# Two hidden units of the second feed-forward block placed ahead of the first block's output units at the head of each step

## The chip, the cores and the metric

The kernel runs on one NeuronCore of a Trainium2 chip. The metric is the device time of one execution in microseconds (us). Before the change the median of three executions is 3286.47 us (3281.36 to 3291.28).

## The reference, cut to what matters

Two layers run over an image batch `x` of 16 x 96 x 96 x 96 (images, channels, rows, columns). Each layer has a mixer on the image and then a feed-forward block (FFN) on its tokens:

```python
# layer 0
x = x + _L0_conv_ref(_ln_c(x), ...)
t = _to_tokens(x)
t = t + _L0_ffn_ref(_ln_t(t), W1, b1, W2, b2)
# layer 1
x = x + _L1_conv_ref(_ln_c(x))
t = t + _L1_ffn_ref(_ln_t(t), W1, b1, W2, b2)

def _ffn_ref(x, W1, b1, W2, b2):
    h = relu(_qlinear(x, W1, b1))     # 96 -> 384 hidden
    return _qlinear(h, W2, b2)        # 384 -> 96
def _qlinear(x, W, b):
    y = q_acc(einsum('bsk,nk->bsn', q_mul(x), q_mul(W)))   # operands in 8 bit, sums in 16 bit
    return q_acc(y + q_mul(b))
```

The mixer of layer 0 compares every 3 x 3 patch with 512 vectors (the scores), takes the best match and sends it through a small multilayer network (the MLP). The mixer of layer 1 divides by a power of a 5 x 5 window sum.

## The kernel before, in words

The image is cut into 128 tiles of 128 patches with 9 pixels each, eight tiles to an image. All engines walk through the same list of 145 **steps**, and in one step each engine works on several tiles at different stages (`PARTS`, line 63): the scores of tile k+3 (`f1`), the match of k+2 (`f2`), the MLP of k+1 (`f3`), the first layer of FFN 0 of tile k (`back`), its second layer for tile k-1 (`tail`), the input of FFN 1 for tile k-11 (`pre`) and both layers of FFN 1 for tile k-12 (`rear`). Nothing is scheduled by a program: the order in which each engine does its part of a step is written out by hand in the `body` functions, TensorE's at lines 488 to 545 and ScalarE's at lines 623 to 681. An engine works strictly in that order, so an instruction that waits holds back everything written after it. Every eighth step (k % 8 = 1) window sums are added and in the one after it VectorE computes the factors of an image.

One FFN tile is 11 **units** on TensorE, numbered 0 to 10 (`fill`, line 379). Units 0 to 8 are hidden units: one matrix product each (line 393), of 512, 512 and 128 columns in turn. Units 9 and 10 are the output units: 15 and 12 products (line 401) that need the finished hidden tile. Each FFN owns two banks of PSUM and unit u uses bank u % 2. ScalarE copies each unit out (`take`, line 565): hidden units to `ffn_hid`, output units to `ffn_y` (both line 553). A unit may be filled when the unit two before it has been copied out.

Three things gate an FFN tile. ScalarE writes the normalised input `ffn_x` (`norm`, line 586). SyncE's queue (SP) then issues a DMA that transposes it into `ffn_xT` (`turn`, line 331); unit 0 waits for it to land (line 387). VectorE adds bias and ReLU to the hidden tile in three parts (line 898) and rounds it (line 906, the **round-up**); the first output unit waits for that (line 398). For FFN 1 the input of a tile is written near the end of step k-1, the transpose is issued there, behind the store of an output tile (line 348) and the loads of the next `xt` (line 325) and `xc` (line 318), and the hidden units run in step k. For FFN 0 the hidden units run at the end of step k-1, the round-up is VectorE's last work of that step, and the output units run at the head of step k.

At the head of a step TensorE does, in this order: two scores (line 416), FFN 0's unit 9, one score, FFN 1's unit 0, FFN 0's unit 10, FFN 1's units 1 and 2, then the transpose of the MLP's input (line 434). ScalarE copies that to `inpT`; `win_turn` (line 423) and `mlp_in` (line 439) wait for `inpT`, and from there on TensorE goes in one row through scores, `mlp_mid` (lines 445 and 447), `win_scores` (line 429) and the rest of FFN 1's hidden units to `mlp_last` (line 453), `conv` (line 461) and FFN 0's hidden units. ScalarE also computes `x3` at the head (`lrn_pixels`, line 599, nine pixels in a step), and its copies of the units stand in an order of their own between these.

Of the kernel before, what the change touches and what calls it, by code (L numbers as in the profile page):

```python
# [116 lines left out]
def build(nc, x_tok, x_chan, wm_in, wi1_in, wi1r_in, wi2_in, wl1_in, wl2_in, wconv_in, bmlp_in, ffn_in, shift_in,  # L117
# [4 lines left out]
    with ctx:  # L122
# [116 lines left out]
        ffn0, ffn1 = Ffn("ffn0", 0, 4), Ffn("ffn1", 1, 6)  # L239
# [121 lines left out]
        def _(pe):  # L361
# [44 lines left out]
            def score(f1, f2, p, j0, j1):  # L406


                if j0 == 0:
                    pe.wait_ge(xc_loaded[p], landed(f1, p))  # L410
                for j in range(j0, j1):

                    pe.wait_ge(score_taken, f1 * J + j + (2 if j == WIN_TURN else 1))
                    if j == WIN_TURN + 1 and f2 is not None:
                        pe.wait_ge(vidx_ready, f2 + 1)
                    last = pe.matmul(ps_score[score_bank(j)], xc[p][:, j, :], wcT[:, :], start=True, stop=True)  # L416
                    last.then_inc(score_ready, 1)

            def win_turn(f2, p):
                pe.wait_ge(win_loaded, (f2 + 1) * 16)  # L420
                wait_past(pe, winT_ready, f2)
                wait_past(pe, inpT_ready, f2)
                pe.transpose(ps_a[0:C, 0:P], win[p][:, :], ident[:, :]).then_inc(win_turned, 1)
# [7 lines left out]
            def mlp_turn(f3):  # L431
                pe.wait_ge(inp_ready, f3 + 1)
                wait_past(pe, x1_ready, f3)
                pe.transpose(ps_a[0:D1, 0:P], inp[:, :], ident[:, :]).then_inc(inp_turned, 1)
# [53 lines left out]
            def body(k):  # L488
                def scores(j0, j1):
                    if k.f1 is not None:  # L490
                        score(k.f1, k.f2, k.q, j0, j1)

                def hidden_units(ffn, tile, first, units):
                    if tile is not None:
                        fill(ffn, tile, k.back_p if ffn is ffn0 else k.rear_p, first, units)

                def out_units(ffn, tile, parity, u):
                    if tile is not None:
                        fill(ffn, tile, parity, HC * G + u, 1)

                scores(0, 2)
                out_units(ffn0, k.tail, k.tail_p, 0)
                scores(2, 3)
                hidden_units(ffn1, k.rear, 0, 1)
                out_units(ffn0, k.tail, k.tail_p, 1)
                hidden_units(ffn1, k.rear, 1, 2)
                if k.f3 is not None:
                    mlp_turn(k.f3)
                hidden_units(ffn1, k.rear, 3, 1)
                if k.f2 is not None:  # L510
                    win_turn(k.f2, k.q)
                if k.lrn is not None:
                    pe.wait_ge(box_ready, k.lrn + 1)
                if k.f3 is not None:
                    mlp_in(k.f3)
                hidden_units(ffn1, k.rear, 4, 1)
                scores(3, WIN_TURN)
                if k.f3 is not None:
                    if k.f2 is not None:
                        pe.wait_ge(winT_ready, k.f2 + 1)  # L520
                    mlp_mid(k.f3)
                hidden_units(ffn1, k.rear, 5, 1)
                if k.f2 is not None:
                    win_scores(k.f1, k.f2)
                hidden_units(ffn1, k.rear, 6, 1)
                scores(WIN_TURN, 5)
                hidden_units(ffn1, k.rear, 7, 1)
                scores(5, 6)
                if k.f3 is not None:
                    mlp_last(k.f3)  # L530
                scores(6, 7)
                hidden_units(ffn1, k.rear, 8, 1)
                if k.f3 is not None:
                    conv(k.f3)
                hidden_units(ffn0, k.back, 0, 2)
                scores(7, 8)
                hidden_units(ffn0, k.back, 2, 3)
                scores(8, J)
                window_sums(k, 0, 5)
                hidden_units(ffn0, k.back, 5, 2)  # L540
                out_units(ffn1, k.rear, k.rear_p, 0)
                window_sums(k, 5, 10)
                hidden_units(ffn0, k.back, 7, 2)
                out_units(ffn1, k.rear, k.rear_p, 1)
                window_sums(k, 10, WINDOW_PARTS)

            steps(body)


        @block.scalar  # L550
        def _(act):
# [39 lines left out]
            def lrn_pixels(k, j0, j1):  # L591

                if k.pre is None:
                    return
                if j0 == 0:
                    act.wait_ge(cols_ready, k.pre + 1)
                    wait_past(act, x4_ready, k.pre - XT + 1)
                for j in range(j0, j1):
                    last = nc.scalar.activation(x3[:, k.pre3, j, :], x2[:, k.pre & RING - 1][:, j, :],  # L599
                                                ACT.Identity, bias=cols[k.q][:, 1, j:j + 1],  # L600
                                                scale=cols[k.q][:, 0, j:j + 1])
                if j1 in (XA, J):
                    last.then_inc(x3_ready, 1)
# [19 lines left out]
            def body(k):  # L623
                def take_hidden(ffn, tile, first, units):
                    if tile is not None:
                        take(ffn, tile, k.back_p if ffn is ffn0 else k.rear_p, first, units)

                def take_out(ffn, tile, parity, u):
                    if tile is not None:
                        take(ffn, tile, parity, HC * G + u, 1)  # L630

                lrn_pixels(k, 0, 3)
                take_out(ffn0, k.tail, k.tail_p, 0)
                lrn_pixels(k, 3, 4)
                take_hidden(ffn1, k.rear, 0, 2)
                if k.f3 is not None:
                    act.wait_ge(inp_turned, k.f3 + 1)
                    copy(inpT[:, :], ps_a[0:D1, 0:P]).then_inc(inpT_ready, 1)
                take_hidden(ffn1, k.rear, 2, 2)
                take_out(ffn0, k.tail, k.tail_p, 1)  # L640
                if k.f2 is not None:
                    act.wait_ge(win_turned, k.f2 + 1)
                    copy(winT[0:C, :], ps_a[0:C, 0:P]).then_inc(winT_ready, 1)
                if k.f3 is not None:
                    act.wait_ge(z1_made, k.f3 + 1)
                    nc.scalar.activation(h[:].rearrange("c m p -> c (m p)"), ps_b[0:C, 0:M1 * P], ACT.Relu,
                                         scale=1.0 - LEAK).then_inc(h_ready, 1)
                take_hidden(ffn1, k.rear, 4, 1)
                norm0(k, 0, 5)
                take_hidden(ffn1, k.rear, 5, 1)  # L650
                if k.f3 is not None:
                    act.wait_ge(z2_made, k.f3 + 1)
                    nc.scalar.activation(vcs[:, :], ps_a[0:C, 0:P], ACT.Tanh,
                                         bias=bmlp[:, 0:1]).then_inc(vcs_ready, 1)
                norm0(k, 5, 7)
                take_hidden(ffn1, k.rear, 6, 1)
                norm0(k, 7, 8)
                take_hidden(ffn1, k.rear, 7, 1)
                if k.f3 is not None:
                    act.wait_ge(z3_made, k.f3 + 1)  # L660
                    for q in range(2):
                        last = nc.scalar.activation(h1[0:LH, q, :], ps_b[0:LH, q * P:(q + 1) * P], ACT.Relu,  # L662
                                                    bias=bmlp[0:LH, 1 + q:2 + q])
                    last.then_inc(h1_ready, 1)
                norm0(k, 8, J)
                take_hidden(ffn1, k.rear, 8, 1)
                lrn_pixels(k, 4, XA)
                norm1(k, 0, 1)
                lrn_pixels(k, XA, 6)
                norm1(k, 1, 3)  # L670
                lrn_pixels(k, 6, 8)
                norm1(k, 3, 4)
                take_hidden(ffn0, k.back, 0, 2)
                lrn_pixels(k, 8, J)
                take_hidden(ffn0, k.back, 2, 3)
                norm1(k, 4, XA)
                norm1(k, XA, 6)
                take_hidden(ffn0, k.back, 5, 4)
                norm1(k, 6, J)
                take_out(ffn1, k.rear, k.rear_p, 0)  # L680
                take_out(ffn1, k.rear, k.rear_p, 1)

            steps(body)


# [576 lines left out]
```

## Time and profile before

| what | value |
|---|---|
| median of three executions | 3286.47 us |
| the profiled execution, its own time | 3290.14 us |
| span of its trace | 3288.4 us |
| TensorE busy (share of the span) | 2775.2 us (84%) |
| VectorE busy | 2900.0 us (88%) |
| ScalarE busy | 2642.5 us (80%) |
| GpSimd busy | 1511.8 us (46%) |
| mean granted TensorE clock | 0.962 |

The rows of the trace name the engines PE (TensorE matrix products), PEld (its weight loads), DVE (VectorE), ACT (ScalarE), POOL (GpSimd) and SP (SyncE, which issues most DMAs). `out<-in` are the program's names with buffer numbers left out: `banks` is PSUM, `x` stands for several pixel tiles, `ffn_x`, `ffn_xT`, `ffn_hid` and `ffn_y` for those of either FFN. A time in brackets is idle time of the engine just before the row and what ended it. Products overlap in the pipeline, so the distance from one start to the next says more than a row's length. The granted clock is a share of 2.4 GHz: 1.00 is that, 0.50 is 1.2 GHz.

### The profile page before, as it was taken

The page shows a single profiled execution, that of the slowest core. Times are in us where ns is not written, and L with a number is a line of the kernel's source. Part 1 is how long each engine was busy: PE and PEld are TensorE (multiplying, and loading weights), DVE is VectorE, ACT ScalarE, POOL GpSimd, SP SyncE. Part 2 cuts the span into 40 slices and gives each one's busy share as a digit, 9 for nine tenths or more (in the row PEclk, how much of TensorE's full clock was granted, in tenths as well). Part 3 has the DMA queues.
Part 4 walks back from the last instruction along what each step waited for, and adds up shares of the span by engine and source line. Part 5 has one row for each costly group of instructions (what it writes and reads, how often), then busy time and mean ns, then how long its engine had stood idle before and what let it go on. Part 6 is the DMA issues. An engine that isn't in the chain of part 4 may idle for free.

```text
span 3288.4 us, 56026 instructions
## 1 busy us (share of the span) xinstructions
PE 2775.2 (84%) x15886; PEld 1493.4 (45%) x15886; DVE 2900.0 (88%) x10715; ACT 2642.5 (80%) x7047; POOL 1511.8 (46%) x1415
## 2 busy tenths in 40 slices
PE   5888988888888998888889898888888888888644
PEld 2444444444444444444445444444444444444322
DVE  6898999999999999999999999998998999999531
ACT  0444988889888898888888898888888888888877
POOL 1333445454545454554545454454544545445342
PEclk9999999999999999999999999999999999999755
DMA  3122223323232323233232323223233232322111
GB/s 91 51 57 58 74 72 76 81 69 86 70 86 70 86 70 85 70 84 71 74 78 76 80 72 84 70 78 75 70 86 70 70 83 70 85 68 61 35 45 48
DMA packets 236608, 237.33 MB, mean 72 GB/s; under 512 B 183426, under 2 KB 186764, under 8 KB 236300
## 3 DMA queue, kind: packets, MB, share of 16 engines
q1 hardware_dynamic: 226060, 214.86, 25.6%
q0 software_dynamic: 10240, 18.89, 2.3%
q8 instruction: 129, 2.11, 0.3%
q14 instruction: 179, 1.47, 0.2%
HBM read 134.72 MB, written 57.02 MB: 58 GB/s over the span
## 4 chain that ended last, share of the span: by engine, by line
PE 35%; ACT 19%; DVE 18%; DMA 12%; issue 5%; POOL 1%; SPq 0%; POOLq 0%; DVEq 0%; ACTq 0%
PE banks L416 12%; DMA ffn_xT<-ffn_x 12%; PE banks L393 8%; ACT ffn_hid L553 7%; ACT ffn_x L586 6%; ACT x L599 4%; PE banks L401 4%; DVE ffn_hid L898 3%; DVE st L810 3%; PE banks L429 3%; DVE pix L819 3%; PE banks L439 2%; PE banks L447 2%; PE banks L453 1%; ACT h L662 1%
## 5 line engine op out<-in xcount | busy, mean ns | idle before, releaser
L553 ACT ACTIVATE ffn_hid<-banks 128x512 f16<-128x512 f32 (+1 forms) x2304 | 1064.6, 489 | 288.5 <-PE banks L393 252.3
L416 PE MATMUL banks<-wcT,xc 128*128 128x512 f32 x2304 | 1190.2, 608 | 44.6 <-DVE vidx L859 21.0
L393 PE MATMUL banks<-ffn_xT,w1q 128*128 128x512 fp8e5 (+1 forms) x2304 | 726.7, 340 | 215.5 <-DMA ffn_xT<-ffn_x 120.1
L819 DVE TENSOR_REDUCE pix<-banks 128x1 f32<-128x512 f32 x1152 | 785.9, 682 | 34.2 <-PE banks L416 21.2
L393 PEld LDWEIGHTS banks<-ffn_xT,w1q 128*128 128x128 bf16 x2304 | 222.8, 98 | 770.7 <-ACT ffn_hid L553 451.0
L401 PE MATMUL banks<-w2q,ffn_hid 128*128 128x96 bf16 x6912 | 391.8, 210 | 204.9 <-DVE ffn_hid L906 204.9
L898 DVE TENSOR_SCALAR ffn_hid<-ffn_hid,b1q 128x1152 f16<-128x1152 f16 x768 | 432.3, 563 | 109.3 <-ACT ffn_hid L553 109.3
L416 PEld LDWEIGHTS banks<-wcT,xc 128*128 128x128 f32 x2304 | 406.5, 192 | 256.7 <-issue 178.0
L1104 POOL TENSOR_TENSOR x<-x,ffn_f 128x864 f32<-128x864 f32 x256 | 480.5, 1877 | 92.3 <-DVE ffn_f L915 90.1
L401 PEld LDWEIGHTS banks<-w2q,ffn_hid 128*128 128x128 f16 x6912 | 350.0, 100 | 345.0 <-issue 314.5
L599 ACT ACTIVATE x<-x,cols 128x96 f32<-128x96 f32 x1152 | 488.2, 460 | 0.0
L586 ACT ACTIVATE ffn_x<-x,cols 128x96 fp8e5<-128x96 f32 x1152 | 476.1, 460 | 4.2
L1118 POOL COPY img<-pix 128x27 f32<-128x27 f32 x128 | 40.3, 315 | 947.4 <-DVE nb L772 767.7
L586 ACT ACTIVATE ffn_x<-x,nb,pix 128x96 fp8e5<-128x96 f32 x1152 | 468.7, 472 | 4.7 <-DVE nb L772 4.7
L810 DVE BATCH_NORM_STATS2 st<-x 128x6 f32<-128x96 f32 x2304 | 425.8, 246 | 5.4 <-POOL x L1104 1.1
L461 PE MATMUL banks<-wc,h 128*128 128x480 f32 (+1 forms) x1024 | 409.1, 543 | 2.2 <-ACT h L662 2.2
L553 ACT ACTIVATE ffn_y<-banks 128x480 f16<-128x480 f32 (+1 forms) x512 | 255.7, 526 | 178.4 <-PE banks L401 178.4
L1086 POOL TENSOR_TENSOR prod_dot<-xt,wrow 128x864 f32<-128x864 f32 x128 | 258.3, 2018 | 210.8 <-DVE ffn_hid L906 185.6
L906 DVE TENSOR_SCALAR ffn_hid<-ffn_hid 128x3456 uint16<-128x3456 uint16 x256 | 274.6, 1073 | 8.9
L461 PEld LDWEIGHTS banks<-wc,h 128*128 128x128 f32 x1024 | 188.2, 194 | 198.6 <-issue 120.5
L1099 POOL TENSOR_TENSOR ffn_f<-ffn_y,b2q 128x864 f16<-128x864 f16 x128 | 235.1, 1837 | 33.6 <-ACT ffn_y L553 31.9
L1070 POOL DMA_INDIRECT win<-x_tok_in,xrow x128 | 126.8, 991 | 262.7 <-DVE xrow L839 262.7
(139 smaller groups left out, 3210.2 us busy)
## 6 DMA issues: line engine op xcount, KB each, us to landing
xt<-x_tok_in SPq DMA_DIRECT2D x128, 432.0 KB, 4.3
xc<-x_chan_in SPq DMA_DIRECT2D x128, 432.0 KB, 5.4
out_tok<-x SPq DMA_DIRECT2D x128, 432.0 KB, 2.8
ffn_xT<-ffn_x SPq DMA_TRANSPOSE x256, 2.8
win<-x_tok_in,xrow POOLq DMA_INDIRECT x128, 4.1
wrow<-vector_table,vidx POOLq DMA_INDIRECT x128, 2.7
shift<-shift_in SPq DMA_DIRECT2D x1, 960.0 KB
vector_table<-wtab SPq DMA_DIRECT2D x1, 384.0 KB, 2.9
```

The costliest lines, as they stand in the source:

```text
L393: last = pe.matmul(bank[:, 0:c1 - c0], w1q[:, ffn.layer, c * P:(c + 1) * P], pairs, start=True, stop=True)
L401: last = pe.matmul(bank[:, (j - j0) * C:(j - j0 + 1) * C], ffn.hid[:, c, j * P:(j + 1) * P], w2q[:, ffn.layer, c, :], start=(c == 0), stop ...
L416: last = pe.matmul(ps_score[score_bank(j)], xc[p][:, j, :], wcT[:, :], start=True, stop=True)
L461: last = pe.matmul(bank[:, 0:(j1 - j0) * C], h1[:, q, :], wc[:, q, j0 * C:j1 * C], start=(q == 0), stop=(q == 1))
L553: return nc.scalar.activation(dst, src, ACT.Copy)
L586: last = nc.scalar.activation(ffn.x8[:, j // 2, 0:C, j % 2], x[:, j, :], ACT.Identity, bias=bias_c[:, j:j + 1], scale=scale_c[:, j:j + 1], ...
L599: last = nc.scalar.activation(x3[:, k.pre3, j, :], x2[:, k.pre & RING - 1][:, j, :], ACT.Identity, bias=cols[k.q][:, 1, j:j + 1], scale=co ...
L810: last = nc.vector.bn_stats(st3[:, which, j, :], src[:, j, :])
L819: nc.vector.tensor_reduce(mx[p][:, j:j + 1], ps_score[score_bank(j)], AX.X, ALU.max).then_inc(score_taken, 1)
L898: nc.vector.tensor_scalar(ffn.hid[:, c, :], ffn.hid[:, c, :], b1q[:, ffn.layer, c:c + 1], 0.0, ALU.add, ALU.max).then_inc(ffn.rounded, 1)
L906: nc.vector.tensor_scalar(bits, bits, TO_E5M2, TO_E5M2, ALU.add, ALU.subtract).then_inc(ffn.hid_ready, 1)
L1104: tt(dst, x, ffn.f[:, :, :], ALU.add).then_inc(ready, 1)
```

## The change

On TensorE FFN 1's hidden units 0 and 1 move from behind the third score to directly behind the first two scores, ahead of FFN 0's unit 9. Unit 10 of FFN 0 then follows the third score, and unit 2 of FFN 1 follows that. On ScalarE the copies of units 0 and 1 move in between the first three pixels of `lrn_pixels`, ahead of the copy of FFN 0's unit 9; the copy of unit 10 moves from behind unit 3 to ahead of unit 2 and of `inpT`. No instruction is added or removed; the queues of VectorE, GpSimd and SyncE keep their order.

```diff
@@ TensorE, body
                 scores(0, 2)
+                hidden_units(ffn1, k.rear, 0, 2)
                 out_units(ffn0, k.tail, k.tail_p, 0)
                 scores(2, 3)
-                hidden_units(ffn1, k.rear, 0, 1)
                 out_units(ffn0, k.tail, k.tail_p, 1)
-                hidden_units(ffn1, k.rear, 1, 2)
+                hidden_units(ffn1, k.rear, 2, 1)
                 if k.f3 is not None:
                     mlp_turn(k.f3)
                 hidden_units(ffn1, k.rear, 3, 1)
@@ ScalarE, body
-                lrn_pixels(k, 0, 3)
+                lrn_pixels(k, 0, 1)
+                take_hidden(ffn1, k.rear, 0, 1)
+                lrn_pixels(k, 1, 2)
+                take_hidden(ffn1, k.rear, 1, 1)
+                lrn_pixels(k, 2, 3)
                 take_out(ffn0, k.tail, k.tail_p, 0)
                 lrn_pixels(k, 3, 4)
-                take_hidden(ffn1, k.rear, 0, 2)
+                take_out(ffn0, k.tail, k.tail_p, 1)
+                take_hidden(ffn1, k.rear, 2, 1)
                 if k.f3 is not None:
                     act.wait_ge(inp_turned, k.f3 + 1)
                     copy(inpT[:, :], ps_a[0:D1, 0:P]).then_inc(inpT_ready, 1)
-                take_hidden(ffn1, k.rear, 2, 2)
-                take_out(ffn0, k.tail, k.tail_p, 1)
+                take_hidden(ffn1, k.rear, 3, 1)
```

TensorE before, at the head of a step in the middle of the run (the products from `ffn_xT` are FFN 1's hidden units 0 to 2, those from `ffn_hid` FFN 0's units 9 and 10):

```order
L416 MATMUL banks<-wcT,xc 128x512 x2
L401 MATMUL banks<-w2q,ffn_hid 128x96 x15
L416 MATMUL banks<-wcT,xc 128x512
L393 MATMUL banks<-ffn_xT,w1q 128x512
L401 MATMUL banks<-w2q,ffn_hid 128x96 x12
L393 MATMUL banks<-ffn_xT,w1q 128x512
L393 MATMUL banks<-ffn_xT,w1q 128x128
L434 MATMUL banks<-ident,inp 106x128
```

TensorE at the same place after the change:

```order
L416 MATMUL banks<-wcT,xc 128x512 x2
L393 MATMUL banks<-ffn_xT,w1q 128x512 x2
L401 MATMUL banks<-w2q,ffn_hid 128x96 x15
L416 MATMUL banks<-wcT,xc 128x512
L401 MATMUL banks<-w2q,ffn_hid 128x96 x12
L393 MATMUL banks<-ffn_xT,w1q 128x128
L434 MATMUL banks<-ident,inp 106x128
```

The first product that needs the transposed input of FFN 1 now stands ahead of unit 9, the third score and unit 10 instead of behind the first two of these.

ScalarE before, at the head of the same step (`x` from `x,cols` is `lrn_pixels`, `ffn_hid` the copies of hidden units, `ffn_y` those of output units):

```order
L599 ACTIVATE x<-x,cols 128x96 x3
L553 ACTIVATE ffn_y<-banks 128x480
L599 ACTIVATE x<-x,cols 128x96
L553 ACTIVATE ffn_hid<-banks 128x512 x2
L553 ACTIVATE inpT<-banks 106x128
L553 ACTIVATE ffn_hid<-banks 128x128
L553 ACTIVATE ffn_hid<-banks 128x512
L553 ACTIVATE ffn_y<-banks 128x384
L553 ACTIVATE winT<-banks 96x128
```

ScalarE there after the change:

```order
L599 ACTIVATE x<-x,cols 128x96
L553 ACTIVATE ffn_hid<-banks 128x512
L599 ACTIVATE x<-x,cols 128x96
L553 ACTIVATE ffn_hid<-banks 128x512
L599 ACTIVATE x<-x,cols 128x96
L553 ACTIVATE ffn_y<-banks 128x480
L599 ACTIVATE x<-x,cols 128x96
L553 ACTIVATE ffn_y<-banks 128x384
L553 ACTIVATE ffn_hid<-banks 128x128
L553 ACTIVATE inpT<-banks 106x128
L553 ACTIVATE ffn_hid<-banks 128x512
L553 ACTIVATE winT<-banks 96x128
```

Between the copy of unit 0 and the copy of `inpT` there was one copy of a unit; there are now three pixels of `lrn_pixels` and four copies of units.

## Rows read from the trace of the kernel before

**Rows 1.** Waits, from 389 to 3045 us: who, for whom: us, times, longest.
```profile
PE banks L401 <- DVE ffn_hid L906: 146.3, 111, 2.5
PE banks L393 <- DMA ffn_xT<-ffn_x: 78.4, 94, 2.2
```
**Rows 2.** Timeline of VectorE, one step: start us, us, line, operation.
```profile
1715.77 1.06 DVE L906 TENSOR_SCALAR ffn_hid<-ffn_hid 128x3456 uint16<-128x3456 uint16 x1
```
**Rows 3.** Timeline of TensorE, head of the step that follows it.
```profile
1716.98 0.80 PE L401 MATMUL banks<-w2q,ffn_hid 128*128 128x96 bf16 x15 [1.30 <-DVE ffn_hid L906]
1717.61 1.09 PE L416 MATMUL banks<-wcT,xc 128*128 128x512 f32 x2
1718.84 0.38 PE L393 MATMUL banks<-ffn_xT,w1q 128*128 128x512 fp8e5 x1
1719.06 0.67 PE L401 MATMUL banks<-w2q,ffn_hid 128*128 128x96 bf16 x12
1719.56 0.57 PE L393 MATMUL banks<-ffn_xT,w1q 128*128 128x512 fp8e5 x2
1720.00 0.29 PE L434 MATMUL banks<-ident,inp 128*106 128x128 f32 x1
...
1721.01 0.82 PE L439 MATMUL banks<-inpT,wi 106*96 106x128 f32 x6
```
**Rows 4.** Chain of waits, three stretches: start us, us, what.
```profile
1711.10 0.86 PE banks L416 x2
...
1714.97 3.73 DMA ffn_xT<-ffn_x
...
2826.72 5.42 DMA ffn_xT<-ffn_x
```
**Rows 5.** Steps, by windows: us, busy of PE, PEld, DVE, ACT, POOL, clock, DMA.
```profile
1716.83:1739.52 22.69, 20.58 (x120) 10.86 (x120) 21.44 (x82) 20.35 (x56) 11.46 (x9) 1.00 0.30 83
2828.34:2852.71 24.37, 20.42 (x120) 10.93 (x120) 21.39 (x82) 20.73 (x56) 11.06 (x9) 1.00 0.34 77
1646.23:1671.88 25.65, 21.49 (x120) 11.76 (x120) 21.41 (x82) 20.48 (x55) 11.08 (x9) 0.93 0.33 72
2194.73:2220.82 26.09, 21.02 (x120) 10.93 (x120) 25.78 (x104) 20.54 (x55) 10.82 (x9) 1.00 0.27 66
1810.96:1839.97 29.01, 24.31 (x120) 12.15 (x120) 25.93 (x104) 20.45 (x55) 10.81 (x9) 0.88 0.26 71
3161.00:3288.00 127.00, 57.43 (x338) 27.92 (x335) 23.58 (x36) 94.95 (x245) 38.00 (x28) 0.50 0.16 50
```
**Rows 6.** Timeline of ScalarE, the same head as in rows 3.
```profile
1715.67 1.18 ACT L599 ACTIVATE x<-x,cols 128x96 f32<-128x96 f32 x3
1717.81 0.57 ACT L553 ACTIVATE ffn_y<-banks 128x480 f16<-128x480 f32 x1 [0.97 <-PE banks L401]
...
1719.25 1.32 ACT L553 ACTIVATE ffn_hid<-banks 128x512 f16<-128x512 f32 x2 [0.52 <-PE banks L393]
1720.47 0.27 ACT L553 ACTIVATE inpT<-banks 106x128 f32<-106x128 f32 x1
...
1721.55 0.48 ACT L553 ACTIVATE ffn_y<-banks 128x384 f16<-128x384 f32 x1
...
1722.45 0.61 ACT L553 ACTIVATE ffn_hid<-banks 128x512 f16<-128x512 f32 x1
```
**Rows 7.** DMA issues and landings: timeline of SP; transfers by issue; transposes of five.
```profile
1712.82 0.63 SPq L318 DMA_DIRECT2D xc<-x_chan_in  x1
...
xc<-x_chan_in SPq DMA_DIRECT2D x1, 432.0 KB, 5.1
...
DMA to landing us min/median/max: 2.4/3.1/3.7
```
**Rows 8.** Timeline of TensorE: unit 0 of FFN 1 in two other steps.
```profile
1650.34 0.58 PE L393 MATMUL banks<-ffn_xT,w1q 128*128 128x512 fp8e5 x1 [2.23 <-DMA ffn_xT<-ffn_x]
...
3178.18 1.01 PE L393 MATMUL banks<-ffn_xT,w1q 128*128 128x512 fp8e5 x2 [3.76 <-DMA ffn_xT<-ffn_x]
```

## The prediction

> **What bounds the kernel now.** I read the waits first, then the head of one step on TensorE and ScalarE, then the chain of waits, then the length of whole steps.
>
> TensorE stops at two places of a step's head. Unit 9 of FFN 0 waits for VectorE's round-up, 146 us in 111 steps, and hidden units wait for a transpose, 78 us in 94 places [rows 1]. The first stop is what the change fills: two units that don't need the round-up go in front of it. But they need the transpose, so the question is which of the two comes first. In the step shown the round-up ends at 1715.77 + 1.06 = 1716.83 [rows 2] and unit 9 starts at 1716.98 [rows 3]. The transpose of FFN 1 is issued at 1714.97 and lands 3.73 later, at 1718.70 [rows 4]; unit 0 starts at 1718.84 [rows 3]. So the transpose is the later one, by 1.87 us. I took the same difference from all 112 steps in which both FFNs and the scores run: never below 0.85, median 2.26, largest 3.97. It is late because the load of `xc`, issued at 1712.82, lands 5.1 us later, at 1717.9, and the transpose follows it [rows 7].
>
> Is that arrival on the path that sets the end? The chain of waits goes through it [rows 4], and step lengths say how much: a step runs here from round-up to round-up. With the landing 1.87 us after the round-up the step takes 22.69 us; with 2826.72 + 5.42 = 2832.14, which is 3.80 us after, it takes 24.37 [rows 4, 5]. 1.93 us later costs 1.68. A line through all 80 ordinary steps at full clock has a slope of 0.96. The step is a loop: landing, head, MLP, FFN 0's hidden units, FFN 1's normalised input, next transpose. Whatever lies between the landing and the MLP adds to each step.
>
> **The change part by part.**
>
> *The round-up's wait.* TensorE will stand in front of unit 0 until the transpose lands, and by then the round-up is long done. The 146 us go, but into one longer wait: 1.30 us in front of unit 9 [rows 3] becomes 1718.84 less (1716.98 - 1.30), so 3.16 us in this step, and 2.6 to 5.5 over the 112. That wait by itself costs nothing, since unit 0 starts where it did.
>
> *What is now behind unit 0 on TensorE.* Before, from unit 0 to the MLP's transpose (L434): 1720.00 - 1718.84 = 1.16 us. After, start to start: unit 0 0.22, unit 1 0.22, unit 9 0.63 (1716.98 to 1717.61), the third score 0.86 [rows 4], unit 10 0.50 (1719.06 to 1719.56), unit 2 0.10 (a quarter of the columns, an estimate) [rows 3]. Sum 2.53, so L434 comes 1.37 later. Unit 9 and the third score, which ran while the transpose was under way, now run after it.
>
> *What is now behind unit 0 on ScalarE.* The MLP goes on when `inpT` is copied. Before, the copy of unit 0 starts at 1719.25 and that of `inpT` at 1720.47 [rows 6], and L439 at 1721.01 [rows 3]. Now ScalarE has between them what the order shows. Consecutive instructions start about 0.1 before the one ahead ends (three pixels take 1.18 [rows 6], 0.36 each and 0.1 over), so each counts its length less 0.1: unit 0 0.51, a pixel 0.36, unit 1 0.51, a pixel 0.36, unit 9 0.47, a pixel 0.36, unit 10 0.38, unit 2 0.17 (taken as the small copy of `inpT`) [rows 6]. Sum 3.12: `inpT` starts at 1722.37, 1.90 later than now, and after TensorE's L434, which ends at 1721.66. ScalarE sets it; the three pixels used its wait for the landing and now come behind it. From L439 on TensorE's order is what it was. Bounds: 1.37, if ScalarE's part were hidden, and 1.90. I take **1.9 per step**, by these rows.
>
> *What else moves.* Unit 10 was copied behind unit 3 and is now copied before `inpT`; measured from L439 that is earlier, so VectorE's bias of FFN 0 and GpSimd's `x2` behind it wait for nothing new. VectorE's maximum of the third score comes up to 1.5 us later, but before the copy of `inpT` and so before ScalarE needs what follows it: nothing. SP's order is the same, and its loads hang on the end of the step, which moves as a whole: the landing keeps its distance from the round-up. The copies of units 0 and 1 take and free the same two banks as before: nothing.
>
> *TensorE's clock.* In the step with 2.23 us of wait before unit 0 [rows 8] the granted clock is 0.93 in the mean, so 25.65 x 0.07 / 0.5 = 3.6 us at 1.2 GHz; its landing is at about 1650.20, 3.97 after the round-up, which at full clock would make 24.37 + 0.15 = 24.52. It took 25.65: such a spell costs 1.1 us. The step at 1810.96 has a mean of 0.88, 7.0 us at 1.2 GHz, and takes 29.01 against 26.09 of its like at 1.00: 2.9 us [rows 5]. In the last steps a wait of 3.76 us stands in every one [rows 8], and the clock is 0.50 throughout [rows 5]. Now every step gets one wait of 2.6 to 5.5 us. Bounds: 0 (the clock holds, as in the step at 2828.34 with its two shorter waits [rows 5]) and 2.9. I take **1.7 per step**, between 1.1 and 2.9, since most of the new waits are longer than the 2.23 that had a spell and near the 3.76 that never lost it.
>
> The Trainium skill (TensorE: Matmul & The Clock Gate, the section "HAM oscillation — how this bites in real kernels") tells of a kernel whose wait for a DMA throttled TensorE anew in every tile, and prices it at half of the throttled time. By that, 3.6 us and 7.0 us would cost 1.8 and 3.5, and the sum would lie 10 to 176 us higher; the two steps above measured 1.1 and 2.9, and these decide.
>
> *The sum.* 98 ordinary steps x (1.9 + 1.7) = 353 us. 14 steps, each eighth, are held by VectorE (busy 25.78 of 26.09 [rows 5]) and hide part of the shift: 2.0 each, between 0 and 3.6, gives 28. Four steps without scores: unit 9 and unit 10 behind the landing, about 1 each, 4. Ten last steps have no FFN 0, but three pixels, 1.08 us, move behind the landing on ScalarE, of which I take 0.7: 7. Together 392. On the profiled execution's own 3290.1 us that makes 3682; it stands 3.7 above the median, so I predict **3678 us**, 11.9% slower.
>
> **The rivals.**
>
> *The clock holds.* Only the arrival counts: 98 x 1.9 + 14 x 1 + 11 = 211, so 3498 us; with TensorE's 1.37 alone about 3445. For it: the wait is only one in a step of some 25 us, and TensorE is busy about 90% of a step [rows 5]. Against it: rows 8. Chance 0.18.
>
> *A long spell in every step.* 98 x (1.9 + 2.9) + 14 x 3 + 11 = 523, so about 3810 us. For it: a spell that begins inside the wait loses part of its time doing nothing and may be renewed, as in the last steps. Chance 0.13.
>
> *The transpose comes earlier and the change pays.* The place is unit 0 of FFN 1. The shortest transposes take 2.4 us [rows 7]; at that the landing is at 1717.37, 0.5 after the round-up, instead of 2.4 in the mean. L439 would then come at landing + 2.3 + 1.9 = 4.7 us after the round-up, against 2.4 + 2.3 = 4.7 now: no change. Faster begins below 0.5; with the landing at the round-up it is 0.5 x 98 = 49 us, 3237. The price is right, but of 112 landings none came below 0.85, and the load of `xc` stays ahead of it. Chance 0.03.
>
> *The head doesn't matter.* If another path set the step, nothing would change: 3286. Against it the slope of 0.96. Chance 0.02.
>
> **How the numbers follow.** My forecast has 0.64; its own range is 3600 to 3760, for 1.0 to 2.4 us of clock per step. The range of 8 in 10 reaches down to the case in which the clock holds at 1.9, so 3490 to 3760; it leaves out the long spells, the earlier transpose and TensorE's 1.37 alone. A measurement of this kernel can tell about 0.3%, 10 us, from no change. Faster by more than that 0.03, within 0.02, slower 0.95.
>
> **What would show it.** Right: unit 0 waits for the transpose in nearly every step, 2.6 to 5.5 us, and the wait for the round-up in front of unit 9 is gone; from landing to L439 4.2 us instead of 2.3; `inpT` is copied right behind unit 2; granted clock of the steady part about 0.93 to 0.87 instead of 0.99; steps of 25 to 27 us. Wrong: a landing less than 1 us after the round-up (SP's loads moved), a clock that stays at 1.00 in most steps (the time is then near 3500), or `inpT` early in spite of the copies ahead of it.

## The result, and the profile after

The changed kernel takes 3625.6 us in the median (3623.0 to 3634.0, four executions) against 3288.9 us (3281.4 to 3293.8) before: the ratio is 1.101, 95% interval 1.098 to 1.103. It is 10% slower; the prediction said 3678 us, with 3490 to 3760 as its range. The profiled execution takes 3627.8 us.

The page of the changed kernel, span and engines:

```profile
span 3626.1 us, 56026 instructions
PE 2892.6 (80%) x15886; PEld 1590.6 (44%) x15886; DVE 2918.9 (80%) x10715; ACT 2640.5 (73%) x7047; POOL 1517.3 (42%) x1415
```

The number of instructions is the same. VectorE is busy 19 us longer than before and ScalarE 2 us shorter; TensorE is busy 117 us longer, and that with the same products. The waits of TensorE in the steady part of the changed kernel (400 to 3380 us; who, for whom: us, times, longest):

```profile
PE banks L393 <- DMA ffn_xT<-ffn_x: 422.7, 126, 5.7
PE banks L423 <- ACT inpT L553: 63.1, 111, 0.8
```

These answer to [rows 1]. The wait for the round-up (146 us) is gone from the list, as the change intends. The wait for the transpose has grown from 78 to 423 us, and a wait for `inpT` is new. The same head of a step as in [rows 3], in a step of the changed kernel whose clock is full (timeline of TensorE; the round-up ended at 1901.48, the landing below is from the chain of waits):

```profile
1899.87 3.18 DMA ffn_xT<-ffn_x
```

```profile
1903.18 0.59 PE L393 MATMUL banks<-ffn_xT,w1q 128*128 128x512 fp8e5 x2 [2.62 <-DMA ffn_xT<-ffn_x]
1903.61 0.80 PE L401 MATMUL banks<-w2q,ffn_hid 128*128 128x96 bf16 x15
1904.25 1.09 PE L416 MATMUL banks<-wcT,xc 128*128 128x512 f32 x2
1905.18 0.67 PE L401 MATMUL banks<-w2q,ffn_hid 128*128 128x96 bf16 x12
1905.69 0.22 PE L393 MATMUL banks<-ffn_xT,w1q 128*128 128x128 fp8e5 x1
1905.74 0.27 PE L434 MATMUL banks<-ident,inp 128*106 128x128 f32 x1
...
1907.18 0.82 PE L439 MATMUL banks<-inpT,wi 106*96 106x128 f32 x6
```

The transpose lands at 1903.05, 1.57 us after the round-up, and only then do units 0 and 1, unit 9, the score, unit 10 and unit 2 follow. L434 starts 2.69 us after the landing (before: 1.30). ScalarE in that step (timeline, as [rows 6]):

```profile
1903.60 0.60 ACT L553 ACTIVATE ffn_hid<-banks 128x512 f16<-128x512 f32 x1 [2.57 <-PE banks L393]
1904.09 0.46 ACT L599 ACTIVATE x<-x,cols 128x96 f32<-128x96 f32 x1
...
1905.28 0.57 ACT L553 ACTIVATE ffn_y<-banks 128x480 f16<-128x480 f32 x1
1905.73 0.47 ACT L599 ACTIVATE x<-x,cols 128x96 f32<-128x96 f32 x1
1906.09 0.49 ACT L553 ACTIVATE ffn_y<-banks 128x384 f16<-128x384 f32 x1
1906.46 0.29 ACT L553 ACTIVATE ffn_hid<-banks 128x128 f16<-128x128 f32 x1
1906.62 0.30 ACT L553 ACTIVATE inpT<-banks 106x128 f32<-106x128 f32 x1
```

From unit 0's copy to that of `inpT` it works without a break for 3.02 us, where it took 1.22 before. TensorE has finished L434 at 1906.01 and waits: ScalarE sets `inpT` here. In a step whose clock is down, it is the other way round. TensorE, then ScalarE, in the step from 2036.70 (landing at 2039.63):

```profile
2039.77 1.01 PE L393 MATMUL banks<-ffn_xT,w1q 128*128 128x512 fp8e5 x2 [4.24 <-DMA ffn_xT<-ffn_x]
2040.58 1.41 PE L401 MATMUL banks<-w2q,ffn_hid 128*128 128x96 bf16 x15
2041.78 2.04 PE L416 MATMUL banks<-wcT,xc 128*128 128x512 f32 x2
2043.61 1.17 PE L401 MATMUL banks<-w2q,ffn_hid 128*128 128x96 bf16 x12
...
2044.68 0.42 PE L434 MATMUL banks<-ident,inp 128*106 128x128 f32 x1
```

```profile
2044.82 0.49 ACT L553 ACTIVATE ffn_y<-banks 128x384 f16<-128x384 f32 x1 [1.82 <-PE banks L401]
...
2045.36 0.28 ACT L553 ACTIVATE inpT<-banks 106x128 f32<-106x128 f32 x1
```

The score takes 1.83 from start to start instead of 0.93, L434 comes 5.05 us after the landing, and ScalarE waits 1.82 us for unit 10. The windows of the steady part, of these two steps and the one ahead of the first of them, and of a stretch near the start (columns as [rows 5]):

```profile
400.00:3380.00 2980.00, 2444.07 (x13740) 1356.30 (x13738) 2506.61 (x9189) 2279.24 (x6110) 1315.37 (x1224) 0.93 0.27 68
1874.88:1901.48 26.60, 21.82 (x120) 11.91 (x120) 21.62 (x82) 20.60 (x55) 11.07 (x9) 0.94 0.26 70
1901.48:1925.86 24.38, 20.17 (x120) 10.91 (x120) 21.48 (x82) 20.49 (x55) 11.36 (x9) 1.00 0.32 75
2036.70:2064.15 27.45, 22.72 (x120) 12.42 (x120) 21.58 (x81) 20.50 (x55) 11.08 (x9) 0.88 0.30 65
235.00:388.00 153.00, 133.22 (x626) 72.70 (x627) 127.53 (x511) 85.09 (x224) 51.56 (x58) 0.90 0.19 50
```

The clock was 0.99 over the steady part before:

```profile
400.00:3045.00 2645.00, 2323.37 (x13671) 1260.42 (x13669) 2473.56 (x9143) 2270.79 (x6082) 1304.44 (x1219) 0.99 0.30 76
```

For all kernels the table has means over the same 98 steps (both FFNs and scores at work, without every eighth step that VectorE holds), worked out from the traces: from the round-up to the landing, from there to the start of the copy of `inpT`, and the rest of the step, which is its length less the two.

| kernel | time, us | steady clock | step, us | landing | to `inpT` | rest |
|---|---|---|---|---|---|---|
| before | 3288.9 | 0.99 | 23.51 | 2.36 | 1.81 | 19.34 |
| changed | 3625.6 | 0.93 | 26.59 | 2.45 | 4.83 | 19.31 |
| e1, TensorE's order alone | 3583.7 | 0.93 | 26.17 | 2.41 | 4.44 | 19.32 |
| e2, ScalarE's order alone | 3571.6 | 0.96 | 26.16 | 2.36 | 3.62 | 20.18 |
| e8, e2 with extra products | 3509.5 | 0.99 | 25.50 | 2.40 | 3.61 | 19.49 |
| e3, changed with extra products | 3487.2 | 1.00 | 25.37 | 2.37 | 3.68 | 19.32 |
| e4, changed, `xc` behind | 3400.7 | 0.97 | 24.54 | 1.07 | 4.13 | 19.34 |
| e9, e3 and e4 together | 3340.7 | 1.00 | 24.02 | 1.10 | 3.59 | 19.33 |
| e5, before, `xc` behind | 3211.1 | 1.00 | 22.73 | 1.13 | 2.28 | 19.32 |
| e6, units behind the MLP | 3249.5 | 1.00 | 23.20 | 2.48 | 0.59 | 20.13 |
| e7, e5 and e6 together | 3234.1 | 1.00 | 23.03 | 1.18 | 1.84 | 20.01 |

The last column is the main finding. Whatever the head does, the rest of the step takes 19.3 us, except where the rest itself was touched (e2, e6, e7, e8). So the time is read off the two columns ahead of it. 14 of the 98 are the steps that add window sums: there the rest takes 22.0 us and in the other 84 it takes 18.9, so a single step without window sums is about half a microsecond shorter than the mean in the table (in e5 the 84 take 22.28). For e1 to e4, e8 and e9 the time is that of one execution; beside them the kernel before took 3289 to 3305 us in single executions.

### The profile page after: what moved, and what is told of

Read it like the earlier page. It is cut to its first block, busy times and chain, and to the rows that moved or that the text cites. A ratio compares the mean times of both kernels' runs of the same rounds, so it can differ in the third digit from the quotient of the medians.

```text
span 3626.1 us, 56026 instructions
## 1 busy us (share of the span) xinstructions
PE 2892.6 (80%) x15886; PEld 1590.6 (44%) x15886; DVE 2918.9 (80%) x10715; ACT 2640.5 (73%) x7047; POOL 1517.3 (42%) x1415
## 4 chain that ended last, share of the span: by engine, by line
PE 28%; DMA 17%; POOL 16%; issue 15%; ACT 11%; DVE 9%; SPq 3%; POOLq 0%; DVEq 0%
DMA ffn_xT<-ffn_x 15%; PE banks L416 10%; POOL x L1108 7%; PE banks L393 5%; PE banks L401 4%; POOL prod_dot L1090 4%; ACT ffn_hid L553 4%; ACT ffn_x L586 3%; POOL ffn_f L1103 3%; ACT x L599 3%; DVE pix L823 2%; SPq L318 2%; POOL wrow L1082 2%; PE banks L461 1%; PE banks L439 1%
## 5 line engine op out<-in xcount | busy, mean ns | idle before, releaser
L416 PE MATMUL banks<-wcT,xc 128*128 128x512 f32 x2304 | 1259.8, 640 | 32.6 <-DVE pix L823 19.5
L393 PE MATMUL banks<-ffn_xT,w1q 128*128 128x512 fp8e5 (+1 forms) x2304 | 738.2, 353 | 541.6 <-DMA ffn_xT<-ffn_x 480.5
L401 PEld LDWEIGHTS banks<-w2q,ffn_hid 128*128 128x128 f16 x6912 | 429.0, 113 | 240.1 <-issue 180.5
L416 PEld LDWEIGHTS banks<-wcT,xc 128*128 128x128 f32 x2304 | 425.4, 201 | 242.6 <-issue 171.3
L599 ACT ACTIVATE x<-x,cols 128x96 f32<-128x96 f32 x1152 | 515.6, 459 | 0.0
L401 PE MATMUL banks<-w2q,ffn_hid 128*128 128x96 bf16 x6912 | 463.7, 230 | 45.9 <-DVE ffn_hid L910 45.9
L1082 POOL DMA_INDIRECT wrow<-vector_table,vidx x128 | 128.9, 1007 | 304.8 <-DVE vidx L863 294.3
(139 smaller groups left out, 3234.1 us busy)
```

The costliest lines, as they stand in the source:

```text
L393: last = pe.matmul(bank[:, 0:c1 - c0], w1q[:, ffn.layer, c * P:(c + 1) * P], pairs, start=True, stop=True)
L401: last = pe.matmul(bank[:, (j - j0) * C:(j - j0 + 1) * C], ffn.hid[:, c, j * P:(j + 1) * P], w2q[:, ffn.layer, c, :], start=(c == 0), stop ...
```

## Experiments

The theory going in was the prediction's: the landing, what stands behind it on TensorE and ScalarE, and the clock. Rivals were that one engine's order does it alone, that the clock spells cost nothing, and that the transpose is late for another reason than `xc`.

**One engine's order alone.** e1 takes TensorE's order of the change and leaves ScalarE's:

```diff
                 scores(0, 2)
+                hidden_units(ffn1, k.rear, 0, 2)
                 out_units(ffn0, k.tail, k.tail_p, 0)
                 scores(2, 3)
-                hidden_units(ffn1, k.rear, 0, 1)
                 out_units(ffn0, k.tail, k.tail_p, 1)
-                hidden_units(ffn1, k.rear, 1, 2)
+                hidden_units(ffn1, k.rear, 2, 1)
```

> TensorE's order of the change, ScalarE's order of before. Theory (landing, plus ScalarE's pixels, plus the clock): in the changed kernel L434 starts 4.1 us after the landing at a clock that is half down, and the copy of inpT follows it; ScalarE's chain of 3.1 us is hidden behind that. So TensorE's order alone brings nearly all of the loss: 3580 to 3625 us, a granted clock of about 0.91, L434 at about 4.1 us after the landing. Rival (the copies and pixels ahead of inpT are what costs): most of it goes, 3290 + 98 x 1.4 = about 3430 us or less.

It took 3583.7 us with a steady clock of 0.93. That is 42 us less than the change, and L434 starts 4.1 us after the landing in both. So TensorE's order with its clock brings almost nine tenths of the loss by itself, and ScalarE's order on top of it 0.42 us per step. ScalarE adds this at either clock: `inpT` starts 0.04 us after the end of L434 in e1, and in the changed kernel 0.60 after it in steps at full clock and 0.3 to 0.4 in steps with a spell at half clock, since copies of units stand between. The rival, that the copies and pixels alone are the cost, is out.

e2 is the reverse, ScalarE's order with TensorE's order of before:

```diff
-                lrn_pixels(k, 0, 3)
+                lrn_pixels(k, 0, 1)
+                take_hidden(ffn1, k.rear, 0, 1)
+                lrn_pixels(k, 1, 2)
+                take_hidden(ffn1, k.rear, 1, 1)
+                lrn_pixels(k, 2, 3)
                 take_out(ffn0, k.tail, k.tail_p, 0)
                 lrn_pixels(k, 3, 4)
-                take_hidden(ffn1, k.rear, 0, 2)
+                take_out(ffn0, k.tail, k.tail_p, 1)
+                take_hidden(ffn1, k.rear, 2, 1)
...
-                take_hidden(ffn1, k.rear, 2, 2)
-                take_out(ffn0, k.tail, k.tail_p, 1)
+                take_hidden(ffn1, k.rear, 3, 1)
```

> ScalarE's order of the change, TensorE's order of before. Theory: TensorE waits twice as before, the clock stays near 0.96, and inpT is copied 1.9 us later behind the landing than before (3.7 us instead of 1.8): 98 x 1.9 + 14 + 11 = 211, about 3500 us. Rival (only TensorE's order counts, ScalarE has room): within 10 us of the kernel before, 3280 to 3300.

It took 3571.6 us, 71 more than the theory gave, and far from the rival. So ScalarE's order brings over four fifths of the loss by itself too: either order alone holds `inpT` back, and the two losses don't add up. `inpT` is at 3.6 us after the landing, as expected; but the rest of the step is 0.85 us longer and the steady clock 0.96. The windows of e2's steady part, TensorE's waits in it, and a step's head:

```profile
400.00:3330.00 2930.00, 2431.94 (x13753) 1334.14 (x13751) 2493.64 (x9182) 2289.09 (x6122) 1308.76 (x1226) 0.96 0.27 69
```

```profile
PE banks L423 <- ACT inpT L553: 174.2, 111, 1.6
PE banks L401 <- DVE ffn_hid L910: 148.9, 111, 3.1
PE banks L393 <- DMA ffn_xT<-ffn_x: 78.9, 100, 2.4
```

```profile
1712.47 0.39 PE L393 MATMUL banks<-ffn_xT,w1q 128*128 128x512 fp8e5 x1 [0.45 <-ACT ffn_hid L553]
1714.44 0.29 PE L423 MATMUL banks<-ident,win 128*96 128x128 f32 x1 [1.58 <-ACT inpT L553]
1714.56 0.82 PE L439 MATMUL banks<-inpT,wi 106*96 106x128 f32 x6
...
1715.44 1.83 PE L416 MATMUL banks<-wcT,xc 128*128 128x512 f32 x2
1717.06 0.63 PE L445 MATMUL banks<-inpT,leak 106*96 106x128 f32 x2
1717.49 1.48 PE L447 MATMUL banks<-h,wi 96*96 96x128 f32 x6
```

TensorE stands for 1.6 us in front of L423 in every step, and here the products behind it run slow: the six products of L447 take 1.48 us, and the six of L439 just ahead, still at full clock, 0.82. e8 fills just that wait of e2 with two more score products, in the steps without the factors of an image:

```diff
                 hidden_units(ffn1, k.rear, 3, 1)
+                if k.f1 is not None and k.f3 is not None and k.rear is not None and k.lrn is None:
+                    for _ in range(2):
+                        pe.matmul(ps_b[:, :], xc[k.q][:, 0, :], wcT[:, :], start=True, stop=True)
                 if k.f2 is not None:
                     win_turn(k.f2, k.q)
```

> ScalarE's order of the change alone, with two more score products (1.7 us, overwritten by mlp_in) in front of win_turn, where TensorE waits for inpT. Theory (ScalarE's order costs 1.8 us per step by itself and the rest of its 2.7 is the clock, lost in that new wait): granted clock 0.95 to 0.97, inpT still 3.6 us behind the landing, 3470 to 3500 us. Rival (the rest is something else that ScalarE's order delays, not the clock): 3560 to 3590 us.

It took 3509.5 us, 9 above the range expected. Its steady part:

```profile
400.00:3270.00 2870.00, 2521.72 (x14139) 1357.75 (x14137) 2493.91 (x9182) 2274.84 (x6121) 1305.39 (x1225) 0.99 0.28 70
```

62 of the 71 us come back, the clock is 0.99 and the rest of the step 19.49; the 0.15 us that stay over 19.34 lie ahead of `win_turn`, which starts 0.61 us after `inpT` where it started 0.42 before. So most of the miss in e2 was the clock.

**The clock.** e3 puts three score products into the changed kernel's wait for the transpose, on a bank that L434 overwrites:

```diff
                 scores(0, 2)
+                if k.f1 is not None and k.f3 is not None and k.rear is not None:
+                    wait_past(pe, x1_ready, k.f3)
+                    for _ in range(3):
+                        pe.matmul(ps_a[:, :], xc[k.q][:, 0, :], wcT[:, :], start=True, stop=True)
                 hidden_units(ffn1, k.rear, 0, 2)
```

> The changed kernel with three more score products (2.6 us) in front of unit 0, while TensorE waits for the transpose; their result is overwritten by L434. Theory (clock spells cost 1.1 to 1.2 us of the 3.0 per step): the granted clock goes back to 0.96 to 0.98, L434 comes 2.7 and inpT 3.7 us behind the landing, and the time falls to 3490 to 3530 us in spite of the added work. Rival (the spells lie in time that TensorE waits anyway, and all of the 3.0 us is the order): 3610 to 3650 us, whatever the clock does.

It took 3487.2 us, 3 below the range expected. Windows of its steady part, then TensorE and ScalarE in one head (landing at 1988.97):

```profile
400.00:3240.00 2840.00, 2571.61 (x14428) 1397.78 (x14427) 2501.58 (x9194) 2270.44 (x6109) 1333.69 (x1223) 1.00 0.28 71
```

```profile
1985.04 2.74 PE L505 MATMUL banks<-wcT,xc 128*128 128x512 f32 x6
1989.11 0.59 PE L393 MATMUL banks<-ffn_xT,w1q 128*128 128x512 fp8e5 x2 [1.33 <-DMA ffn_xT<-ffn_x]
...
1991.67 0.27 PE L434 MATMUL banks<-ident,inp 128*106 128x128 f32 x1
```

```profile
1992.55 0.30 ACT L557 ACTIVATE inpT<-banks 106x128 f32<-106x128 f32 x1
```

With 2.7 us of added work in front of the same landing the clock is back at 1.00, L434 comes 2.70 and `inpT` 3.58 us after the landing, and the kernel is 138 us shorter than the change. That is the clock's part: 1.22 us per step. The changed kernel itself agrees: in those 23 of its 98 steps that have no spell at half clock `inpT` comes 3.57 us after the landing. What remains, 25.37 - 23.51 = 1.86 us per step, is the order. The rival is out.

**Why the transpose is late.** e4 (on the changed kernel) and e5 (on the kernel before) let SP issue it ahead of the load of `xc`:

```diff
-                load(Step(k.k + 1))
+                nxt = Step(k.k + 1)
+                if nxt.fs is not None:
+                    load_tokens(nxt.fs, nxt.p)
                 if k.pre is not None:
                     turn(ffn1, k.pre)
+                if nxt.fs is not None:
+                    load_pixels(nxt.fs, nxt.p)
```

> The changed kernel, with SP issuing the transpose of FFN 1 ahead of the load of xc instead of behind it. Theory (the transpose lands late because it follows the load of xc): it lands 0.5 to 1.0 us after the round-up instead of 2.4, TensorE's wait shrinks by 1.5 to 1.9 us, and the clock comes back in part: 3330 to 3430 us. Rival (the transpose is late by itself, or through SP): landing and time as in the changed kernel, 3610 to 3640 us.

> The kernel before, with SP issuing the transpose of FFN 1 ahead of the load of xc. Theory (in the kernel before the landing sets the step whenever it is over 1.57 us behind the round-up): the landing comes about 1.0 us behind it, unit 0 no longer waits, L434 starts 2.9 us after the round-up and ordinary steps take 22.1 to 22.3 us: 3290 - 98 x 0.9 = 3190 to 3215 us. Rival (VectorE, busy 21.4 of 22.7 us, or the later load of xc sets the step instead): 3270 to 3295 us.

e4 took 3400.7 us, e5 3211.1 us (3206.7 to 3212.3, ratio to before 0.974, interval 0.972 to 0.977). SP's timeline in e5, the landing of its transpose (transfers by issue) and two steps:

```profile
1871.39 0.38 SPq L325 DMA_DIRECT2D xt<-x_tok_in  x1
1873.98 1.20 SPq L335 DMA_TRANSPOSE ffn_xT<-ffn_x  x1
1875.24 0.57 SPq L318 DMA_DIRECT2D xc<-x_chan_in  x1
```

```profile
ffn_xT<-ffn_x SPq DMA_TRANSPOSE x1, 2.7
```

```profile
1853.69:1875.84 22.15, 20.27 (x120) 11.02 (x120) 21.30 (x82) 20.49 (x56) 11.37 (x9) 1.00 0.30 83
1875.84:1897.97 22.13, 20.27 (x120) 11.02 (x120) 21.29 (x81) 20.48 (x56) 11.36 (x9) 1.00 0.30 82
```

The transpose takes 2.7 us here instead of the 3.7 of [rows 4] and lands 1.1 us after the round-up in the mean, in either kernel, a little later than expected. Over the 112 steps its mean time from issue to landing falls from 4.3 us before to 3.0 in e5, and it is issued 2.0 us ahead of the round-up in both: the transfer got shorter, not earlier. Whether the load of `xc` held it back by standing ahead of it in SP's queue or by taking its share of the DMA engines is not shown, since no run puts the two on different queues. e5 beats both kernels: where the landing is no longer waited for, steps are 22.1 us long. The rival (late by itself) is out, and so is VectorE as the bound of ordinary steps before: it is busy 21.3 us in these.

e9 takes both helps together, on the changed kernel, with two extra products instead of three:

> The changed kernel with both helps: SP's transpose ahead of the load of xc, and two more score products (1.7 us, overwritten by L434) while TensorE waits in front of unit 0. Theory (what is left is the order itself): landing about 1.0 us behind the round-up, clock 0.96 or more, inpT 3.7 us behind the landing, so 4.7 behind the round-up against 3.4 in the kernel before with the same load: ordinary steps 23.3 to 23.6 us, 3325 to 3350 us. Rival (with an early landing the order costs nothing, and what e4 lost against e5 was the clock): 3200 to 3230 us.

It took 3340.7 us, with steps of 24.02 in the mean and 23.56 without window sums. Against e5 the order alone costs 1.29 us per step, with an early landing and a full clock; `inpT` comes 4.69 after the round-up against 3.41. The steps with the earliest landings, 0.19 us after the round-up in e9 and 0.02 in e5:

```profile
2752.77:2775.33 22.56, 21.16 (x124) 11.73 (x124) 21.39 (x82) 20.38 (x55) 11.37 (x9) 1.00 0.26 77
```

```profile
2640.30:2662.44 22.14, 20.27 (x120) 11.02 (x120) 21.30 (x81) 20.47 (x55) 11.37 (x9) 1.00 0.27 79
```

Here too `inpT` comes later with the change, 3.76 us after the round-up against 3.34. So the order cost time in every landing measured behind the round-up, down to 0.19 us.

**The opposite of the change.** e6 puts units 0 and 1 behind L434, 2 and 3 behind L439, 4 and 5 behind `mlp_mid`, with ScalarE in the same order; e7 adds e5's order on SP. TensorE's part:

```diff
                 scores(2, 3)
-                hidden_units(ffn1, k.rear, 0, 1)
                 out_units(ffn0, k.tail, k.tail_p, 1)
-                hidden_units(ffn1, k.rear, 1, 2)
                 if k.f3 is not None:
                     mlp_turn(k.f3)
-                hidden_units(ffn1, k.rear, 3, 1)
+                hidden_units(ffn1, k.rear, 0, 2)
...
-                hidden_units(ffn1, k.rear, 4, 1)
+                hidden_units(ffn1, k.rear, 2, 2)
...
-                hidden_units(ffn1, k.rear, 5, 1)
+                hidden_units(ffn1, k.rear, 4, 2)
```

> The opposite of the change: FFN 1's units 0 to 2 go behind the MLP's transpose (units 0 and 1 behind L434, 2 and 3 behind L439, 4 and 5 behind mlp_mid), ScalarE in the same order, SP as before. Theory (the landing costs only what stands behind it): L434 starts 2.9 us after the round-up or earlier, whenever the landing comes, inpT 0.5 after it, ordinary steps 22.1 to 22.5 us: 3180 to 3230 us. Rival (the units are late then, and VectorE's ReLU or win_turn behind unit 0 waits for them): 3280 us or more.

> Both: FFN 1's units 0 to 2 behind the MLP's transpose, and SP's transpose ahead of the load of xc. Theory: each alone takes the landing off the path, so the two together bring little over the better one: 3170 to 3210 us. Rival (they add up, because a landing that is early also lets units 0 to 3 and their copies run ahead of the MLP): under 3150 us.

e6 took 3249.5 us (ratio 0.986, interval 0.983 to 0.989), e7 3234.1 us (0.981, 0.978 to 0.984). They are 1.4% and 1.9% shorter than the kernel before, neither reaches what was expected, and e7 is slower than e5. The landing is indeed off the path: `inpT` comes 3.0 to 3.1 us after the round-up, 0.3 to 0.4 earlier than in e5. But the rest of the step is 20.0 to 20.1 us. Three units that had run ahead of L434 now stand behind it, between L434 and `conv`, two of 512 and one of 128 columns: by the 0.22 of [rows 3] for one of 512, an estimated 0.5 us of the 0.7 to 0.8. All of the difference lies between `inpT` and the start of `conv` (8.48 us in e6 and 8.37 in e7, against 7.67 before); what of it is more than the three units was not taken apart.

## Why the prediction was right

*The place.* Right. Unit 0 waits for the transpose and the round-up's wait vanished; the landing kept its distance from the round-up (2.45 us against 2.36).

*The order, 1.9 us per step.* Right: 1.86 in e3, where only it is left. Its parts too: L434 2.69 us after the landing where 2.53 + 0.14 were summed, and ScalarE's row of copies 3.02 where 3.12 were. That ScalarE's row sets `inpT` holds at full clock only; where the clock is down it waits for TensorE's unit 10. With both orders at work ScalarE's share over TensorE's is 0.42 per step (e1).

*The clock, 1.7 us per step.* The right mechanism, too large a term: 1.22, from e3. It had been set between a single spell (1.1) and a double one (2.9), as if nearly every step had one. By the records of the granted clock in the changed kernel's trace, 23 of the 98 steps have no spell at half clock, 46 a single and 29 a double; the steps at 1901.48, 1874.88 and 2036.70 above are one of each. `inpT` comes 3.57, 4.91 and 5.69 us after the landing in the three groups, so a single spell costs 1.34 and a double one 2.12. So the price of a single spell was somewhat low, that of a double one too high, and nearly a quarter of the steps have neither. The 2.9 had been read from the step at 1810.96 [rows 5], whose spell begins only at 1824.32 and covers scores and `conv`, not the wait at the head. Over 98 steps the term is 47 us of the 52 by which the prediction was too high.

*Half of the throttled time.* The same records give 3.6 us at half clock per step. By the price of the Trainium skill (TensorE: Matmul & The Clock Gate, "HAM oscillation — how this bites in real kernels") an estimated 1.8 of them would be lost. The runs say 1.22 and decide. Two reasons show in the trace. 0.44 us of the 3.6 fall ahead of the landing, where TensorE stands anyway. And in the row of `inpT` at 2045.36 TensorE is late, but most of ScalarE's row of copies, which sets `inpT` at full clock, is hidden behind it.

*The small terms.* In the profiled execution: 98 steps give 26.59 - 23.51 = 3.08 each, 302 us (353 predicted). The 14 steps held by VectorE give 28.12 - 26.73 = 1.39 each, 19 us (28). Behind them 4 us were added (11). The first steps brought 12 us (0 predicted), which by luck about makes up for the two terms that came out small: from 235 to 388 us the clock was 0.90 where it had been 1.00, in steps most of which have no unit of FFN 1 yet. TensorE's order is untouched there. e1, e3, e4 and e5 also have spells in that stretch; why the changed kernel has more is open.

*The rivals.* That the kernel gets faster when the transpose comes earlier would have needed a landing below 0.5 us behind the round-up, by this rival's sum; by the table's means it is 2.36 + 1.81 - 3.59 = 0.58. e9 has it at 1.10. But that sum sets an early landing under the change against the late one before, so it prices the landing and not the change. At like landings, e9 against e5, the change costs 1.29 per step, and it would pay only with the transpose ahead of the round-up, since 3.59 is more than 3.41. The rival of a clock that holds is what e3 made by hand: 3487 us where 3498 were given.

*The slope of 0.96.* The trace gives it only where the landing is late: 0.95 over the 76 steps at full clock, without window sums, whose landing is more than 1.4 us behind the round-up. With the six earlier ones it is 0.86, since five of the six stay at 22.1 us. As hardly any landing of the changed kernel is that early, the sum doesn't suffer.

## What to carry to other kernels

Before work is moved into a wait, ask what it needs itself, and compare the two arrivals step by step: here the round-up is there 2.4 us ahead of the transpose, so the move swapped a short wait for a longer one and put 1.9 us of other work behind it. In an order written by hand, work goes in the order in which its inputs arrive, and the place to look for time is the late arrival (one transfer moved on SP's queue: 2.6% faster). A wait of TensorE costs more than its length where the products behind it then run at half clock, as here by 1.22 us per step.

## What was not expected

Filling a wait with useless products made the kernel faster twice: 2.7 us of them per step took 138 us off the changed kernel (3.8%), 1.7 us took 62 off e2. And the clock does not need one long wait to fall: in e2 TensorE's stops are about 1.3, 0.8 and 1.6 us in the mean, with work and a stop of 0.45 in between, and its steady clock was 0.96, against 0.99 in e8, where the last of them is filled.
